# A fused expert, attention and feed-forward kernel: weighted values of a row in one burst, the gate rectified by ScalarE, three feed-forward steps moved one pass later, and new issue orders

## The reference

```
gp    = leaky(x @ w_gate[e])            # leaky(v) = v if v >= 0 else 0.01 v ; 8 routed experts, 1 shared
y     = sum over the top two experts of weight * ((gp * (x @ w_up[e])) @ w_down[e])  +  shared expert
x1    = x + layernorm(banded(q k^T) v)  # q, k, v = y @ W_qkv + b ; no softmax, 32-token band
q, kv = split(ln(x1) @ Wq), ln(x1) @ Wkv            # 16 query heads of 64, one key/value head
sim   = 8 * l2norm(q) q_scale . l2norm(k) k_scale + position bias, masked, with one null key
attn  = softmax(sim) @ v                            # the weighted values
z     = ln(attn @ Wout)
h     = silu(z w1) * (z w2);  h = gelu(h h1);  h = gelu(h h2)
out   = x1 + h w3
```

## Time and profile before

| | |
|---|---|
| median of 3 runs | 865.01 us (864.04 to 866.01) |
| the profiled execution | 863.99 us, of which the span of its trace is 861.9 us |
| busy, share of the span | PE 94%, PEld 70%, DVE 70%, ACT 72%, POOL 53% |
| mean granted TensorE clock | 0.990 of full speed |
| the passes in the span | prologue 0 to 73.7 us, group 0 to 147.2 us, six steady passes to 739.1 us, last pass to 836.8 us, drain to 861.9 us |

### The profile page before, as it was taken

The page is one execution under the profiler, slowest core; times in us unless marked ns, Lnnn a source line. Parts: engine busy times, 40 slices in busy tenths (PEclk is TensorE's granted clock), DMA queues, the critical chain, the costliest instruction groups (busy, mean ns, idle before and its releaser), DMA issues. The chain is left out here.

```text
span 861.9 us, 16913 instructions
## 1 busy us (share of the span) xinstructions
PE 806.7 (94%) x5368; PEld 604.3 (70%) x5368; DVE 605.4 (70%) x1621; ACT 617.3 (72%) x1660; POOL 453.8 (53%) x388
## 2 busy tenths in 40 slices
PE   4988989999999999999999999999999999799987
PEld 3765566677766778577766768577776777577877
DVE  5878898967678666967668676876668676665522
ACT  2425776589748987498857987499856897498854
POOL 3128767754573565554584374645665365863210
PEclk9999999999999999999999999999999999799999
DMA  7041100000100001000010001000010000000000
GB/s 242 1 129 60 50 2 29 1 1 1 30 12 2 1 1 42 1 2 1 1 41 1 2 1 41 1 2 1 1 41 1 2 2 14 1 1 1 14 6 7
DMA packets 15589, 16.99 MB, mean 20 GB/s; under 512 B 1408, under 2 KB 13072, under 8 KB 15120
## 3 DMA queue, kind: packets, MB, share of 16 engines
q1 hardware_dynamic: 15504, 15.92, 5.8%
HBM read 13.81 MB, written 2.11 MB: 18 GB/s over the span
## 5 line engine op out<-in xcount | busy, mean ns | idle before, releaser
L605 POOL TENSOR_TENSOR sb_sm<-sb_sm,sb_rden 128x512 f32<-128x512 f32 x128 | 135.8, 1064 | 253.4 <-DVE sb_rden L1070 252.8
L699 ACT ACTIVATE sb_sm<-sb_sm,sb_nmx 128x129 f32<-128x129 f32 x512 | 199.1, 393 | 25.9 <-DVE sb_nmx L1065 24.3
L598 POOL TENSOR_TENSOR sb_biasm<-sb_bias,sb_maskn 128x512 f32<-128x512 f32 x128 | 164.8, 1301 | 13.7 <-issue 5.7
L1057 DVE SCALAR_TENSOR_TENSOR sb_sm<-ps_S,sb_rq,sb_biasm 128x129 f32<-128x129 f32 x512 | 143.5, 343 | 37.7 <-PE ps_S L1289 29.5
L1289 PEld LDWEIGHTS ps_S<-sb_k,sb_qs 64*128 64x128 f32 x1024 | 69.2, 189 | 58.5 <-issue 56.9
L1289 PE MATMUL ps_S<-sb_k,sb_qs 64*128 64x129 f32 x1024 | 93.2, 300 | 15.0 <-DVE sb_sm L1057 14.2
L588 POOL TENSOR_TENSOR sb_rq<-sb_qss,sb_mhalf 128x16 f32<-128x16 f32 x32 | 93.2, 2936 | 16.3 <-DVE sb_qss L1043 16.3
L699 ACT ACTIVATION_READ_ACCUMULATOR sb_sm<-sb_sm,sb_nmx 128x1 f32 x512 | 96.9, 189 | 0.0
L706 ACT ACTIVATE sb_pT<-ps_T 128x512 f32<-128x512 f32 x128 | 74.8, 592 | 26.4 <-PE ps_T L1297 26.4
L1065 DVE TENSOR_REDUCE sb_nmx<-sb_sm 128x4 f32<-128x516 f32 x128 | 86.0, 678 | 0.8
L1297 PE MATMUL ps_T<-sb_ident,sb_sm 128*128 128x128 f32 x512 | 79.3, 279 | 4.2 <-POOL sb_sm L605 3.6
(11 more groups left out here) (227 smaller groups left out, 1806.4 us busy)
## 6 DMA issues: line engine op xcount, KB each, us to landing
sb_xg<-in_xT SPq DMA_DIRECT2D x8, 256.0 KB, 3.9
sb_xs<-in_x SPq DMA_DIRECT2D x8, 256.0 KB, 4.3
sb_qs<-in_xT SPq DMA_DIRECT2D x1, 2048.0 KB, 10.6
sb_hA<-in_h SPq DMA_DIRECT2D x2, 1024.0 KB, 4.9
out_y<-sb_res SPq DMA_DIRECT2D x7, 256.0 KB, 2.4
sb_sm<-toeplitz SPq DMA_DIRECT2D x1, 1024.0 KB, 5.8
sb_rows<-in_rows SPq DMA_DIRECT2D x1, 648.0 KB, 6.4
sb_oT<-in_wq SPq DMA_DIRECT2D x1, 512.0 KB, 10.4
```

Source lines behind the costliest of these rows:

```text
L598: pool.tensor_tensor(biasm[:, heads, 1:NK], bias0[:, heads], maskn[:, j // 4].unsqueeze(1).broadcast_to([128, 4, S]), ALU.add)\
L605: pool.tensor_tensor(sm[:, heads, 1:NK], sm[:, heads, 1:NK], rden[:, heads].unsqueeze(2).broadcast_to([128, 4, S]), ALU.mult)\
L699: ins = act.activation(sm[:, h], sm[:, h], ACT.Exp, bias=nmx[:, h:h + 1], accum_out=den[:, h:h + 1])
L1057: ins = dve.scalar_tensor_tensor(sm[:, h], bank(g, "sim", j, odd)[:, m * NK:(m + 1) * NK], rq[:, k * HEADS + h:k * HEADS + h + 1], biasm[: ...
```

## The change

Four edits, in one program.

1. `PV` becomes one step for a whole row: the two half rows are issued one after the other, into both T banks, and both wait until all four `PT` of the row have been copied. There are four such steps in a group instead of eight. ScalarE's copies and the `z` steps stay eight.
2. The gate leaves its bank through ScalarE's Prelu with slope 0.01. VectorE's own leaky instruction and its two waits go, five times in each group.
3. Pass 6 gets its own lists ("seventh"), which leave out `l3` parts 2 and 3 and `l4` of group 5. These come in the last pass as `l3p`, `l4p` (stage E, shifted by two groups), together with the store of that group.
4. All other lists are ordered anew, and in the prologue the transfers of the experts' gate and up weights are issued by ScalarE's queue instead of SyncE's. `wd` is fetched earlier.

```
-            def pv(g, n):
-                ps = free(g, "PV", n, 0, (v_shifted, 1), (pt_copied, 2 * n + 2))
-                for odd in range(2):
-                    ins = pe.matmul(ps[DH * odd:DH * (odd + 1)].rearrange("p (h s) -> p h s", h=4), vs[:, n // 2],
-                                    pT[:, n % 2 * 8 + odd:n % 2 * 8 + 8:2], start=True, stop=True)
-                ins.then_inc(pv_psum.sem, 1)
+            def pv(g, k):
+                for n in (2 * k, 2 * k + 1):
+                    ps = free(g, "PV", k, n % 2, (v_shifted, 1), (pt_copied, 4 * k + 4))
+                    for odd in range(2):
+                        ins = pe.matmul(ps[DH * odd:DH * (odd + 1)].rearrange("p (h s) -> p h s", h=4), vs[:, k],
+                                        pT[:, n % 2 * 8 + odd:n % 2 * 8 + 8:2], start=True, stop=True)
+                    ins.then_inc(pv_psum.sem, 1)
...
-        "kv": "M", "q": "M", "ssq": "", "kT": "M", "sim": "SS", "PT": "T", "PV": "T", "zT": "M",
+        "kv": "M", "q": "M", "ssq": "", "kT": "M", "sim": "SS", "PT": "T", "PV": "TT", "zT": "M",
...
-                act.activation(gs[:, c % 2], bank(g, "exp", c, 0)[:], ACT.Copy).then_inc(gate_copied.sem, 1)
+                act.activation(gs[:, c % 2], bank(g, "exp", c, 0)[:], ACT.Prelu, alpha=0.01).then_inc(gate_leaked.sem, 1)
...
             def expert(g, c):
-                dve.wait_ge(gate_copied.sem, gate_copied.at(g, c + 1))
-                dve.scalar_tensor_tensor(gs[:, c % 2], gs[:, c % 2], 0.01, gs[:, c % 2], ALU.mult, ALU.max)\
-                    .then_inc(leaked.sem, 1)
+                dve.wait_ge(gate_leaked.sem, gate_leaked.at(g, c + 1))
                 dve.wait_ge(expert_psum.sem, expert_psum.at(g, 3 * c + 2))
-                dve.wait_ge(leaked.sem, leaked.at(g, c + 1))
...
+LATE = {step + "p": step for step in ("l3", "l4")}
+STAGE |= {step: "E" for step in LATE}
...
-            shift = {"P": 1, "A": 1, "B": 0, "C": -1, "D": 0}[STAGE[step]]
+            shift = {"P": 1, "A": 1, "B": 0, "C": -1, "D": 0, "E": -2}[STAGE[step]]
...
-            fetch("wg", wgu_raw[:, 0])
-            fetch("wu", wgu_raw[:, 1])
+            act.dma_start(wgu_raw[:, 0], a["wg"]).then_inc(load["wg"], 16)
+            act.dma_start(wgu_raw[:, 1], a["wu"]).then_inc(load["wu"], 16)
```

The lists of TensorE for the steady and the last pass:

```
     "pe steady": """
-        rw.0 sim.0 exp.0 sim.1 exp.1 sim.2 exp.2-3 sim.3 exp.4 down.0 zT.0 PT.0 sim.4 PT.1 qkv.0 l1.0 sim.5 l1.1
-        PT.2 l1.2 PT.3 l1.3 sim.6 PV.0-1 sim.7 scores.0 l2.0-2 PT.4 mix.0 z.0 PT.5 sim.8 l2.3 PT.6 sim.9 z.1
-        PV.2 sim.10 l3.0 PT.7 l3.1 sim.11 l3.2 xnT.0 PT.8 z.2 sim.12 PT.9 l3.3 sim.13 PV.3-4 sim.14 PT.10 q.0
-        kv.0 sim.15 q.1 z.3 PT.11 q.2 l4.0 PT.12 q.3 z.4 PV.5 qs.0-3 q.4-5 PT.13 q.6-7 PT.14 qs.4-7 z.5 qst.0
-        PT.15 PV.6-7 kT.0 z.6-7
+        sim.0 rw.0 exp.0 sim.1 exp.1 sim.2 exp.2-4 sim.3 down.0 PT.0 zT.0 PT.1 sim.4 qkv.0 l1.0 PT.2 l1.1-2
+        sim.5 l1.3 PT.3 scores.0 sim.6 PV.0 sim.7 l2.0-1 sim.8 PT.4 l2.2 PT.5 sim.9 l2.3 z.0 sim.10 PT.6 mix.0
+        PT.7 l3.0-1 z.1 sim.11 PV.1 sim.12 PT.8 xnT.0 l3.2 PT.9 sim.13 l3.3 z.2 kv.0 PT.10-11 sim.14 q.0-2 z.3
+        sim.15 PV.2 q.3-4 z.4 qs.0-3 q.5 PT.12 q.6 l4.0 PT.13 z.5 q.7 PT.14-15 qs.4-7 PV.3 kT.0 qst.0 z.6-7
...
     "pe last": """
-        sim.0-4 zT.0 PT.0-1 l1.0 sim.5 l1.1-2 PV.0 l1.3 PT.2 sim.6 z.0 PT.3 sim.7 l2.0 PT.4 l2.1 PT.5 sim.8 l2.2
...
+        sim.0 l3p.2 sim.1 l3p.3 sim.2-3 l4p.0 sim.4 PT.0 zT.0 sim.5 PT.1 l1.0-2 sim.6 PT.2 l1.3 PT.3 l2.0 PV.0
...
```

ScalarE's and VectorE's lists at the start of a steady pass, and VectorE's in the prologue from the last expert on:

```
     "act steady": """
-        xh.0 exp.0 rw.0 exp.1-4 ex.0-2 down.0 zT.0 ex.3 qkv.0 l1.0 PT.0 h1.0 l1.1 PT.1 l1.2 h1.1 PT.2-3 l1.3
+        xh.0 rw.0 exp.0-2 ex.0 exp.3-4 ex.1-2 down.0 PT.0 zT.0 ex.3 qkv.0 PT.1 l1.0-1 h1.0-1 PT.2 l1.2-3 PT.3
...
     "dve steady": """
-        rw.0 xl.0 ln3.0 sim.0 exp.0 sim.1 max.0 exp.1-2 sim.2 exp.3 max.1 exp.4 inv.0 max.2 zT.0 sim.3 inv.1
+        rw.0 xl.0 ln3.0 sim.0 exp.0 sim.1 max.0 exp.1 sim.2 exp.2-3 max.1 inv.0 exp.4 inv.1 max.2 zT.0 sim.3
...
     "dve fill": """
-        down.0 pl.1 rt.8 qkv.0 scores.0 pl.2 mix.0 nk.1 maskn.0 ln1.0 ln2.0 xnT.0 rt.9 q.0-1 kv.0 q.2-4 kT.0
+        down.0 rt.9 pl.1 qkv.0 scores.0 mix.0 nk.1 ln1.0 pl.2 ln2.0 xnT.0 kv.0 q.0-2 maskn.0 q.3 kT.0 q.4-5 pl.3
```

More of the change, by code:

```diff
@@ L51 @@
     "pe fill": """
[L52 to L55, removed]
+        lg.0 warm.0-2 pb.0 warm.3-6 pb.1 warm.7-8 rw.0 lg.1 exp.0 lg.2 exp.1 lg.3 exp.2 lg.4-5 exp.3 lg.6-7
+        exp.4 pb.2 warm.9-10 down.0 warm.11 pb.3 warm.12 qkv.0 scores.0 warm.13 mix.0 fl.0-1 warm.14 fl.2 xnT.0
@@ L56 @@
+        fl.3 kv.0 q.0-2 qs.0 warm.15 q.3-5 qs.1-2 q.6 qs.3-4 q.7 warm.16 kT.0 qs.5-7 warm.17-18 qst.0 warm.19-21
     """,
     "pe start": """
[L58 to L61, removed]
+        sim.0 rw.0 exp.0 sim.1 exp.1 sim.2-3 exp.2 sim.4 exp.3 PT.0 exp.4 down.0 PT.1 sim.5 PT.2-3 sim.6 qkv.0
@@ new lines @@
+        sim.15 PV.2 q.3-4 z.4 qs.0-3 q.5 PT.12 q.6 l4.0 PT.13 z.5 q.7 PT.14-15 qs.4-7 PV.3 kT.0 qst.0 z.6-7
+    """,
+    "pe seventh": """
+        rw.0 sim.0 exp.0 sim.1-2 exp.1-2 sim.3 exp.3 PT.0 exp.4 down.0 sim.4 zT.0 PT.1 qkv.0 l1.0 PT.2 sim.5
+        l1.1 scores.0 l1.2 PT.3 sim.6 l1.3 sim.7 PV.0 l2.0 sim.8 PT.4 mix.0 l2.1 PT.5 sim.9 l2.2 sim.10 PT.6 z.0
+        PT.7 l2.3 sim.11 PV.1 sim.12 l3.0 xnT.0 PT.8 z.1 l3.1 sim.13 PT.9 q.0 PT.10 z.2 sim.14 q.1-2 sim.15
+        PT.11 z.3 kv.0 q.3 qs.0 PV.2 qs.1 q.4-5 PT.12-13 qs.2 q.6 z.4 PT.14 q.7 qs.3 kT.0 qs.4 PT.15 qs.5-7 z.5
+        PV.3 qst.0 z.6-7
@@ L107 @@
+        q.6 ssq.0 ssc.0 q.7 vs.0
     """,
     "dve start": """
[L109 to L112, removed]
@@ L114 @@
+        kT.0 inv.15 q.4-6 pl.5 ssq.0 ssc.0 vs.0 q.7
     """,
     "dve steady": """
[L116 to L119 removed]
@@ L122 @@
     """,
     "dve last": """
[L124 to L128, removed]
+        sim.0 max.0 sim.1 ln3.0 sim.2 max.1 sim.3 inv.0 max.2-3 inv.1-2 zT.0 sim.4 inv.3 zl.0 l4p.0 l1.0 sim.5
@@ L152 @@
     "sp fill": """
-        rw.0 maskn.0 hw.0
+        maskn.0 hw.0 rw.0
     """,
     "sp start": """
-        rw.0 maskn.0 hw.1
+        rw.0 hw.1 maskn.0
     """,
@@ L160 @@
     """,
+    "sp seventh": """
+        maskn.0 rw.0
+    """,
     "sp last": """
-        l4.0 l4d.0
+        l4p.0 l4.0 l4d.0
     """,
@@ L200, in uses @@
     return "MM" if (step, k) == ("exp", NX - 1) else USES.get(step, "")
-PHASES = {-1: "fill", 0: "start", NG - 1: "last", NG: "drain"}
+PHASES = {-1: "fill", 0: "start", NG - 2: "seventh", NG - 1: "last", NG: "drain"}
 def passes(engine):
```

97 lines of the change are left out of this document (62 added, 35 removed).

## The result

The changed kernel takes 853.75 us (median of 4 runs, 852.87 to 853.88) beside 865.51 us (864.04 to 867.41) for the kernel before on the same chip: a ratio of 0.9861, interval 0.984 to 0.9882. The forecast was 839 us with a range of 828 to 855. The sign is right and the time lies in the range, but of 26 us only 11.8 came.

A forecast was written before the change was run, and what follows sets the result against it. The prediction took TensorE, busy 94% of the span, to bound the kernel. Its terms summed to 26.1 us: 837.9 from the profiled 863.99, 839 us from the median 865.01; range 828 to 855.

The forecast's parts named there:

- part 4: New orders: group 0's pass -3.5 us, prologue -1, other steady-pass waits -1.5, last pass from `l1.0` on -0.5.
- Part 1, the gate: Expert stretch of each pass: gate on ScalarE starts `down` at 12.35 instead of 14.41 us; six passes, -12.6 us.
- Part 2, the burst: `PV` on TensorE: two half rows back to back save changes of matmul form; -2 us (0 to -4).
- Part 4, the steady orders: Steady-pass waits beside the expert stretch, reordered: -0.25 us in each of six passes, -1.5 us (+6 to -6).
- Part 4, prologue and first pass: Group 0's pass: fewer TensorE waits, -3.5 us; prologue: broadcast rows issued earlier, -1 us.
- Part 3, the late steps: Last pass's start: feed-forward work moved from pass 6 fills a 9.2 us hole; net -5 us (0 to -8).
- The give-back in pass 6: Pass 6 loses 9.2 us of TensorE work but returns 1.0 us for its softmax chain and 0.5 for `qs`.
- the freed time is taken back: Rival: TensorE meets the next wait, exponentials holding the gate or GpSimd's query norms; 855 us, 18%.
- The rival with a table load of its own: Prelu on ScalarE needs its own table, loads of 1.28 us between the experts; 867 us, 1%.
- the one with a stalling burst: Rival: the first `PT` after each of 32 bursts waits for ScalarE's copies, 1.0 us each; 871 us, 3%.
- The late steps only shift the hole: Rival, last pass: `zT` waits for `l4p` throughout, which costs the late steps' saving; 844 us, inside the range.

The follow-up runs named there:

- e1: The changed kernel with the store of a group's result issued one pass later, behind that pass's loads of mask and x; 850.91 us.
- e6: The kernel before with the gate edit alone (Prelu on ScalarE, VectorE's leaky instruction gone), all lists as before; 854.47 us.
- e4: The changed kernel with the gate undone (ScalarE's Copy and VectorE's leaky instruction back), in the new lists; 875.79 us.
- e5: The changed kernel with half rows in place of bursts, the two halves next to each other in the lists; 853.48 us.
- e11: The changed kernel with half rows, the store behind the next loads and the gate and up weights back on SyncE's queue; 851.17 us.
- e2: The changed kernel with the transfers of the experts' gate and up weights back on SyncE's queue, right behind the conditioning; 853.62 us.
- e10: e11 with the prologue's and the first pass's lists of the kernel before; 845.22 us.
- e7: The changed kernel without the late steps, its seventh pass running the new steady lists; 862.2 us.
- e8: The kernel before with the late steps alone, in its own lists; 873.71 us.
- e13: e10 with two steady-pass exchanges: VectorE's scores 9 ahead of split h2.2, GpSimd's bias 9 ahead of normalising probabilities 3; 866.37 us.
- e9: The kernel before with the gate edit and the late feed-forward steps, in the lists of before; 860.77 us.

## Why the prediction was right in sign and too large

The two profiled spans differ by 10.8 us, where the terms made 26.1. The step that failed is part 4, the price of the new orders, and with it the treatment of the terms as separate prices that add up. By pass lengths the missing 15 us are 5.6 in the prologue and the first pass, 4.1 in the five steady passes, about 3.3 in pass 6 and the last pass with the drain, and the 2.0 of the burst. That the time fell into the range owes something to the range's width. The terms, one by one:

- **Part 1, the gate (12.6 us).** Mechanism and size were right for a pass that nothing disturbs: the stretch is 12.45 us in e1, 12.35 was the walk. The price on ScalarE was right (596 ns, no table loads). What failed is its place in the sum. It was taken as the gate's own; e6 shows 1.2 us a pass in the old order, and e4 that the rest is the new order's, which needs the gate.
- **Part 2, the burst (2 us).** Nothing, twice (e5, e11). In the steady pass neither the feared stall nor the gain shows.
- **Part 4, the steady orders (1.5 us).** For the five steady passes parts 1 and 4 made 11.8 us; they got 7.7 shorter, and 12.1 with the loads ahead of the store: 4.4 us of span went to one queue's order. The prediction walked TensorE, VectorE, ScalarE and GpSimd, and left out SyncE, whose list it took as unchanged. The list is, but its store waits for a step of VectorE's that moved behind, and the loads stand behind the store. In the timed runs e1 gives 2.8 us back, an amount near the edge of what they can tell.
- **Part 4, prologue and first pass (4.5 us).** This term failed most. They came to 1.1 us longer instead: the first matmul 2.0 later, prologue 0.7 longer, first pass 1.6 shorter. I priced the rows' earlier landing, and not that the weights on a second queue slow the small transfer that starts everything; but that is not the main loss, since e2 takes it back and the prologue still ends at 77.3 us. What costs is the prologue's new order: with the same queues and the same clock it ends 2.7 us later than by the old one (e10, e11), and 2.3 us of that stand before the first expert. The forecast had it 1 us shorter. The first pass gained 1.6, where 3.5 were forecast, and the old lists with the gate alone gain 2.4 (71.1, e6): that gain is the gate's, not the new order's. Which step of the prologue's lists costs how much was not tried.
- **Part 3, the late steps (5 us).** Pass 6 got 9.2 us shorter, the gate's share in it, where 10 were summed. The last pass and the drain got 4.7 longer in place of 2.4. Its hole was walked to 1 us: `l1.0` 2.9 later was said, it is 3.9. From there to the last `z` the pass was to get 0.5 shorter and is level (80.3 against 80.2 us), and the drain is 0.7 longer, with 6.8 us of low clock near it, where the kernel before has 3.4. The undone steps measure 8.5 us (e7), since the new last pass without them is worse than the old one.
- **The give-back in pass 6** (1.0 us for the softmax chain and 0.5 for `qs`) came to 2.5: beside an undisturbed steady pass of 96.2, pass 6 has 9.2 us less work and is 6.7 shorter. It is that small only because the seventh pass has lists of its own. In the old ones the give-back is 6.5 us (9.2 less 2.7, e8).

Of the rivals, "the freed time is taken back" gave 855 us and is nearest to the measured number, but for another reason than it names: the exponentials and the query norms did not hold the gate. The time went to SyncE's queue, the prologue's new order and the last pass. The rival with a table load of its own fell by the row above, the one with a stalling burst by e5 and e11. "The late steps only shift the hole" fell by e7.

## What to carry to other kernels

When lists are reordered, walk every queue that has a wait in it, SyncE's too: a store that waits for a late result holds all the loads behind it, and one line of order can outweigh an edit of instructions (e13). An edit that frees an engine and an order that uses it have no separate prices: measure the edit in both orders. When two profiled runs are compared, compare their passes at the same granted clock: a first pass by the same lists took 71.1 to 73.8 us (e6, e9). Before an instruction goes ahead of another, ask what it waits for, not when it ran.
